# A rewritten opening of a two-layer mixture kernel: adapter merges in pairs of batches, conditioned chunks split from PSUM, gating lagged by one chunk

## The reference

```python
hidden_i = x @ wi.T + 2 * (x @ common_wi_a.T) @ common_wi_b.T + expert_lora(x, ids)     # 128 -> 512
cur = relu(hidden_i) @ wo.T + the same two corrections                                   # 512 -> 128
for r in range(4):
    logits = cur @ Wg[r] + bg[r]
    cw = softmax over the two largest of four logits, zero elsewhere
    y[e] = gelu(cur @ W1[e] + b1[e]) @ W2[e] + b2[e]
    cur = cur + sum_e cw[e] * y[e]
x = x + cur
x = x + ffn(lora_by_language(x))
```

## Time and profile before

| | us |
|---|---|
| median of 3 runs | 513.68 (512.76 to 515.19) |
| profiled execution, its own time | 512.37 |
| its span, first to last instruction | 510.6 |

### The profile page before, as it was taken

The page is one execution under the profiler, slowest core; times in us unless marked ns, Lnnn a source line. Parts: engine busy times, 40 slices in busy tenths (PEclk is TensorE's granted clock), DMA queues, the critical chain, the costliest instruction groups (busy, mean ns, idle before and its releaser), DMA issues.

```text
span 510.6 us, 7414 instructions
## 1 busy us (share of the span) xinstructions
PE 499.0 (98%) x2268; PEld 406.0 (80%) x2268; DVE 417.3 (82%) x606; ACT 391.6 (77%) x541; POOL 124.8 (24%) x103
## 2 busy tenths in 40 slices
PE   9989799999999999999999999999999999999997
PEld 7867688778788888778888877888888788788885
DVE  3578999999999999999999999999987567744333
ACT  2454598779788877979888787988888787698653
POOL 3576712122121212112131211214232334310000
PEclk8899999999999999999999999999999999999999
DMA  7700170202022020202202020230202000000001
GB/s 211 189 5 1 39 313 1 84 1 85 0 85 82 1 83 0 83 0 83 82 1 83 0 83 0 83 120 6 83 1 83 1 0 1 1 0 1 0 22 64
DMA packets 6746, 26.30 MB, mean 52 GB/s; under 512 B 2178, under 2 KB 2562, under 8 KB 4546
## 3 DMA queue, kind: packets, MB, share of 16 engines
q1 hardware_dynamic: 6434, 23.11, 13.3%
q0 software_dynamic: 288, 2.88, 1.6%
HBM read 24.81 MB, written 1.18 MB: 51 GB/s over the span
## 4 chain that ended last, share of the span: by engine, by line
PE 53%; DVE 22%; issue 13%; ACT 10%; DVEq 1%; POOL 1%; ACTq 0%; POOLq 0%
PE bank L413 19%; PE bank L414 18%; PE bank L417 11%; ACT act_out L696 6%; DVE hid_lo L923 6%; DVE prod L934 3%; ACT hid_hi L702 3%; DVE chosen L899 2%; PE bank L474 2%; PE bank L441 1%; PE bank L436 1%; DVE logit_lo L870 1%; DVE turned L868 1%; DVE ffn_lo L983 1%; DVE hid_lo L1022 1%
## 5 line engine op out<-in xcount | busy, mean ns | idle before, releaser
L696 ACT ACTIVATE act_out<-bank,vec 128x512 f32<-128x512 f32 x256 | 162.7, 680 | 47.9 <-DVE hid_lo L923 23.7
L923 DVE TENSOR_TENSOR hid_lo<-act_out,hid_hi 128x1024 fp32r<-128x1024 f32 x128 | 161.6, 1283 | 21.5 <-ACT hid_hi L702 21.5
L702 ACT ACTIVATE hid_hi<-act_out 128x1024 fp32r<-128x1024 f32 x128 | 135.9, 1062 | 7.9
L378 POOL TENSOR_TENSOR cur<-cur,prod 128x512 f32<-128x512 f32 x48 | 65.9, 1374 | 240.1 <-DVE prod L934 239.7
L413 PE MATMUL bank<-hid_hi,moe_hi 128*128 128x512 f32 x256 | 100.8, 394 | 2.7 <-DVE hid_lo L923 1.9
L417 PE MATMUL bank<-hid_hi,moe_lo 128*128 128x512 f32 x256 | 99.8, 390 | 0.0
L414 PE MATMUL bank<-hid_lo,moe_hi 128*128 128x512 f32 x256 | 99.7, 390 | 0.0
L414 PE MATMUL bank<-xlo,moe_hi 128*128 128x512 f32 x256 | 99.6, 389 | 0.0
L413 PE MATMUL bank<-xhi,moe_hi 128*128 128x512 f32 x256 | 99.6, 389 | 0.0
L417 PE MATMUL bank<-xhi,moe_lo 128*128 128x512 f32 x256 | 99.6, 389 | 0.0
L413 PEld LDWEIGHTS bank<-hid_hi,moe_hi 128*128 128x128 f32 x256 | 48.0, 188 | 16.9 <-DVE hid_lo L923 4.9
(11 more groups left out here) (118 smaller groups left out, 618.8 us busy)
## 6 DMA issues: line engine op xcount, KB each, us to landing
cw_all<-cw_dram SPq DMA_DIRECT2D x16, 1024.0 KB, 4.7
stage<-ffn_w POOLq DMA_DIRECT2D x1, 2304.0 KB, 9.9
cw_all<-moe_w SPq DMA_DIRECT2D x4, 512.0 KB, 8.3
stage<-lora_all SPq DMA_DIRECT2D x8, 160.0 KB, 7.7
x<-x_t SPq DMA_DIRECT2D x4, 256.0 KB, 6.8
out_t<-x SPq DMA_DIRECT2D x3, 256.0 KB, 2.8
cur<-cond_base SPq DMA_DIRECT2D x1, 512.0 KB, 3.2
stage<-ffn_w POOLq DMA_DIRECT2D x1, 512.0 KB, 4.0
```

The costliest lines, as they stand in the source:

```text
L378: pool.tensor_tensor(cur[:, c, :], cur[:, c, :], prod[:, s % 2, :], ALU.add).then_inc(add_done, 1)
L696: act.activation(act_out[:, f // 2, f % 2, :], bank[:, f, :], ACT.Gelu_apprx_tanh, bias=vec[:, V_B1 + e * FC + f:V_B1 + e * FC + f + 1]).t ...
L702: act.activation(hid_hi[:, s % 2, f - 1:f + 1, :], act_out[:, f // 2, :, :], ACT.Copy)\
L923: dve.tensor_tensor(hid_lo[:, s % 2, 2 * pr:2 * pr + 2, :], act_out[:, pr, :, :], hid_hi[:, s % 2, 2 * pr:2 * pr + 2, :].bitcast(F32), ALU ...
```

## The change

- TensorE merges two batches of one kind at a time (`merge_pair`); the first six merges (kind 0 and kind 1 of batches 0 and 1, kind 0 of batches 2 and 3) stand ahead of the first H and use six banks (6, 7, 4, 5, 2, 3). Then for each pair p: H, H, two merges of kind 1, O, O, two merges of kind 0. The diff below calls merges k, with `merge_of(k)` giving batch and kind.
- The inputs' first chunk and the base weights go over ScalarE's queue; the mixture weights are asked for after all low-rank factors.
- Merged weights pass through six scratch rows (act_out and prod); the language factors load into free rows of `stage`.
- `conditioned(c)` writes `xhi` first; the low part is taken by VectorE from PSUM, no longer by GpSimd from `cur`.
- Gating is one chunk later: `gate_order` for chunk c+2 at e = 3, `gate_choice` for chunk c+1 at e = 0, tanh inside ScalarE's work of e = 1, `gate_weights` at e = 1. The opening does two gate_order, one gate_choice and one gate_weights, where before it did three, three and two.
- GpSimd asks for the FFN weights after its last `moe_lo`.

```diff
-LOAD_AFTER = [0, 1, 3, 4]
-MOE_AT = {0: [0], 1: [1], 2: [2], 3: [3], 5: [4, 5], 6: [6, 7]}
+LOAD_AFTER = {3: 1, 5: 2, 7: 3}
+PAIRS = BATCHES // 2
+FIRST_MERGES = 6
+SCRATCH = 6
...
+            for k in range(0, FIRST_MERGES, 2):
+                merge_pair(k)
+                warm(KEEP_WARM)
+            for p in range(PAIRS):
+                cond_hidden(2 * p)
+                cond_hidden(2 * p + 1)
+                if p < PAIRS - 1:
+                    merge_pair(4 * p + 6)
+                if p == 1:
+                    pe.wait_ge(wg_done, 1)
+                    pe.wait_ge(xs_done, 1)
+                    logits(0, GATE_FIRST)
...
+            def merge_pair(k):
+                b, kind = merge_of(k)
+                if k >= FIRST_MERGES:
+                    pe.wait_ge(merge_free, merge_before(k + 1) + 1)
+                pe.wait_ge(lora_in[b], 16)
+                pe.wait_ge(lora_in[b + 1], 16)
...
+            def conditioned_low(c):
+                dve.wait_ge(cond_xhi, c + 1)
+                dve.wait_ge(cond_cur, c + 1)
+                dve.tensor_tensor(xlo[:, c, :], bank[:, cond_bank(c), :], xhi[:, c, :].bitcast(F32), ALU.subtract)\
+                   .then_inc(xs_done, 1)
...
+            for p in range(PAIRS):
+                relu_low(2 * p)
+                relu_low(2 * p + 1)
+                for k in range(4 * p + 6, min(4 * p + 8, MERGES)):
+                    merged_sum(k)
+                if p + 2 < CHUNKS:
+                    x0_low(p + 2)
+                if p == 0:
                     split_gate()
+                if p == 1:
+                    dve.wait_ge(const_done, CONSTS)
+                    gate_order(0, 0)
+                if p == 2:
+                    gate_choice(0)
+                if p == 3:
+                    gate_weights(0, True)
+                for k in range(4 * p + 8, min(4 * p + 10, MERGES)):
+                    merged_sum(k)
+                if p < CHUNKS - 1:
+                    conditioned_low(p)
+            gate_order(1, 0)
+            conditioned_low(CHUNKS - 1)
             hidden_low(0, 0)
-            gate_choice(CHUNKS - 2)
```

More of the change, by code:

```diff
@@ L367, in mixture_add @@
+            for k in range(FIRST_MERGES):
+                merged_low(k)
+            for p in range(PAIRS):
+                for half, i in enumerate(moe_pieces(p)):
+                    for k in range(4 * p + 2 * half + 6, min(4 * p + 2 * half + 8, 2 * BATCHES)):
+                        merged_low(k)
+                    moe_low(i)
             def mixture_add(rnd, s, last):
@@ new lines, in merge_pair @@
+            def merge_pair(k):
+                b, kind = merge_of(k)
+                if k >= FIRST_MERGES:
+                    pe.wait_ge(merge_free, merge_before(k + 1) + 1)
+                pe.wait_ge(lora_in[b], 16)
+                pe.wait_ge(lora_in[b + 1], 16)
+                for i in range(2):
+                    for fc in range(FC if kind else 1):
+                        rows, half = lora_rows(b + i), b // 4
+                        if kind == 0:
+                            mm = pe.matmul(bank[:, merge_bank(k + i), :], lora[rows, half, 0:D], lora[rows, half, D:D + F],
+                                           start=True, stop=True)
+                        else:
+                            a = D + F + fc * P
+                            mm = pe.matmul(bank[:, merge_bank(k + i), fc * D:(fc + 1) * D], lora[rows, half, a:a + P],
+                                           lora[rows, half, D + 2 * F:LORA_W], start=True, stop=True)
+                        if fc == (FC - 1 if kind else 0):
+                            mm.then_inc(merge_done, 1)
@@ L687, in tanh_gate, with hidden @@
                 act.activation(tanh_gap[:], half_gap[:], ACT.Tanh).then_inc(tanh_done, 1)
-            def hidden(n, s, first=False):
+            def hidden(n, s, first=False, gate=None):
                 e = s % EXPERTS
@@ L703, in hidden @@
                            .then_inc(hi_done, 1)
+                    if f == 1 and gate is not None:
+                        tanh_gate(gate)
             def project_high(c):
@@ new lines, in _ @@
+            for k in range(FIRST_MERGES):
+                merged_high(k)
+                if k == 3:
+                    x0_high(1)
+            for p in range(PAIRS):
+                relu_high(2 * p)
+                relu_high(2 * p + 1)
+                for half, i in enumerate(moe_pieces(p)):
+                    for k in range(4 * p + 2 * half + 6, min(4 * p + 2 * half + 8, MERGES)):
+                        merged_high(k)
+                    moe_high(i)
+                    if half == 0 and p + 2 < CHUNKS:
+                        x0_high(p + 2)
+                if p == 2:
+                    tanh_gate(0)
+                if p < CHUNKS - 1:
+                    conditioned(p)
@@ L943, in round_steps @@
                     n, c, e = STEPS * rnd + s, s // EXPERTS, s % EXPERTS
-                    if s <= EXPERTS + 1:
-                        if e == 1:
-                            gate_weights(CHUNKS * rnd + CHUNKS - 2 + c)
-                    elif e == 1 and not last:
-                        gate_weights(CHUNKS * (rnd + 1) + c - 2)
                     if s < STEPS - 1:
@@ L953, in round_steps @@
                         hidden_low(n + 1, 0)
+                    gated = not (last and c == CHUNKS - 1)
+                    if e == 1 and gated:
+                        gate_weights(CHUNKS * rnd + c + 1)
                     if last and e == 1 and c >= 1:
```

344 lines of the change are left out of this document (134 added, 210 removed).

## The result

| | before | after |
|---|---|---|
| median, us | 514.43 (4 runs, 512.76 to 515.57) | 539.0 (4 runs, 536.85 to 540.93) |
| ratio | | 1.0479, 95% interval 1.0424 to 1.0534 |
| profiled execution, own time | 512.37 | 540.93 |
| its span | 510.6 | 539.1 |
| first expert_out starts | 68.48 | 74.13 |

The change makes the kernel 4.8% slower, more than three times what was forecast and outside the range. The last two lines split the 28.5 us of span: 5.65 are lost in the opening and 22.9 behind it. From its first FFN matmul to the end layer 1 takes 88.5 us against 88.35, so the rounds lost some 22.7 us.

The account below looks back on a forecast made before the run. PE, busy 98% of the span, was taken as the bound, so only its idle and slow stretches count. 4.7 (opening) + 1.5 (clock) + 1.5 (rounds) = +7.7 on 512.4 gave 520.1; predicted median 520.5, range 510 to 527.

Parts of the forecast that it names:

- The start: Opening up to H(0): PE starts at about 6.9, half clock from 9.8, H(0) ends at 21.7, 2.8 us later than before.
- The pairs: Opening's paired batches: PE waits for VectorE and ScalarE, 2.2 and 2.4 us the longest; expert_out(0) at 73.2, +4.7 with the start.
- The clock again: Opening: idles of 2.2 and 2.4 us within 7 us bring one fall of PE's clock, +1.5 us, bounds 0 and 3.
- The low part from PSUM: Opening, VectorE: the subtraction reading PSUM takes 0.67 us; at 1.37 it would add 2.1 in all.
- The rounds: Rounds: moved gating, with tanh in mid-step, costs 0.1 us a chunk over 14 chunks, +1.5, bounds 0 and +12.
- the rounds suffer: Rival: tanh and gate_order at e = 3 make PE wait 0.9 us a chunk, 531 us; chance 0.13.
- Wrong: PE waits of 10 us or more in the rounds: Sign against the forecast: PE waits of 10 us or more in the rounds, at steps with e = 0 or 1.
- The clock holds: Rival: full clock through the opening's merges makes the start 5.4 us better than in the sum, 514.7 us; chance 0.15.
- the opening paced by PE alone: Rival: VectorE keeps up, so the opening's idles and clock fall vanish, 10.7 us off, 509.4 us; chance 0.14.

Follow-up runs that it names:

- o1: e3 with the loads of base and of chunk 0 of x0 moved back to SP's queue: 515.25 us, ratio 1.005 to the kernel before.
- p1: o1 with gate_order(0) behind low halves of batches 4 and 5, gate_choice(0) behind those of 6 and 7, tanh_gate(0) in the first hidden: 513.28 us.
- e1: The changed kernel with only ScalarE's tanh moved from the middle to the end of its step: 521.07 us, ratio 1.017 to the kernel before.
- e3: The changed kernel with tanh at the step's end and gate_order at e=0, gate_choice at e=1, gate_weights at e=2: 517.94 us, ratio 1.011.
- e4: The kernel before with only its tanh moved, into the middle of ScalarE's step behind gate_choice: 522.36 us, ratio 1.017.
- q1: p1 plus split_gate behind the sums of merges 8 and 9, and WARM, KEEP_WARM = 15, 6 for 12, 2: 510.29 us, ratio 0.993.

## Why the prediction was wrong

**The start.** Forecast: half rate from 9.8, clock near 0.5 from 10 to 20 us, H(0) at 19. Measured: 0.50 and 0.50, H(0) at 19.25. That the time is right is luck: two errors cancel. PE was to start at 6.9 and started at 9.04, as the landing was taken from before at 2.7 although x0 and base went to another queue, and o1 shows that this move nearly doubled it. Against that the merges were too dear in the sum. It had 3.8 us for any two at half rate; to the next instruction the pair of kind 1 took 3.03 (12.19 to 15.22) and the second pair of kind 0 took 2.01 (16.37 to 18.38), together 2.6 less. The two merges of the row behind the price were of two kinds and one batch, and the new order puts two batches of one kind side by side.

**The pairs.** H(4) was to start at 42.9 and started at 44.04. Idle ahead of M14: 2.2 forecast, 0.41 measured; ahead of O(4): 2.4 and 2.67; ahead of expert_in: 1.7 and 1.44. The chain is the one described: gate_order(0) on VectorE ahead of sums 12 and 13, and relu_high behind two merged_high on ScalarE; p1, which takes gate_order out of it, has 1.6 us less idle ahead of O(4). The first expert_out was to come at 73.2 (+4.7) and came at 74.13 (+5.65). **The clock again** was to add 1.5. The fall that it was charged for came, at 52.8 behind O(4)'s idle. But the one from 35 us, which before has as well, was twice as long: 0.58 from 35 to 40 us and 0.74 from 40 to 45, 3.4 us of clock, where before had 0.83 over the ten, 1.7. From 24 us to the first expert_out the clock was 0.90 in after and 0.96 in before, 5.0 us against 1.8. The two terms together are 6.2 against 5.65 measured, with errors on both sides in them: the clock cost twice the 1.5, the idles about M10 and the logits were 2.3 in place of 1.0, M14's was 1.8 too long, and the five pairs of merges from M6 to M15 were taken at 2.1 to 2.2 each and took 1.63 and 1.06 in turn, some 3.4 us less, an estimate from the rows above. The chain held; that its sum came within 0.6 us is in part luck, and two profiles of this one opening differ by 1.7.

**The low part from PSUM** was taken at 0.67. It took 0.69. VectorE's timeline after, PSUM's subtraction and then an input's with two SBUF operands:

```profile
35.68 0.69 DVE L879 TENSOR_TENSOR xlo<-bank,xhi 128x512 fp32r<-128x512 f32 x1 [2.26 <-ACT cur L763]
...
41.81 1.48 DVE L856 TENSOR_TENSOR xlo<-x,xhi 128x512 fp32r<-128x512 f32 x1 [1.74 <-ACT xhi L756]
```

**The rounds** are the step that failed. The sum had 0.1 us a chunk over 14 chunks, +1.5, with bounds 0 and +12. Measured: +22.7, of which 1.2 us a chunk, some 18 over the 15 tanhs, and the rest once in the last round, with 3.4 us of clock missing and 2.5 more of PE's wait for GpSimd, which overlap in part. The rival *the rounds suffer* named the tanh together with gate_order, took 0.9 a chunk and gave 531 with 0.13; it had the right mechanism at three quarters of its price and nothing for the last round. The sum went by VectorE's load: 8.4 us of work at e=3 against PE's 5.6. That load was real and was worth 2 to 4 us (e1 to e3). The tanh was dismissed in one sentence without being priced by a row. Its sign could have been seen: a step is four gelus and two high parts on ScalarE (1.23 for two gelus and 1.06 for a high part in the rows above), 4.6 us of PE's 5.6, so it leaves about 1.0; gate_choice, six instructions, takes 2.3 us (199.37 to 201.64) and starts behind the product of the step. A wait of 1.55 us in the middle of ScalarE's step is larger than its slack and comes back every chunk; at the end of the step the same tanh finds its input ready (0.9 us of waiting in all the rounds). It is not the instruction, 0.26 us, but what stands behind it. The size does not come out of this: 1.55 less 1.0 is 0.6 us a chunk, an estimate that lies between the 0.4 of e4 and the 1.2 of after. "Wrong: PE waits of 10 us or more in the rounds" came true: 8.3 for ScalarE, 4.0 and 3.2 for the others, and more on PEld.

**The rivals** of the other side fell with it. *The clock holds* had no case in `after` itself (0.50), *the opening paced by PE alone* neither. They return in part in p1 and q1, with the tanh, the loads and VectorE's order mended (and more warming in q1): the clock is 1.00 from 10 to 20 us and the new opening ends at 65.16 and 65.85, under the 68.48 of the earlier trace rows and the 71.26 of e4. PE still has 5 to 7 us of idle and a fall of the clock behind 24 us in both, so it is not paced by PE alone.

One more thing in the sum: it gives 520.1 for the profiled execution, and with the 1.3 by which the median lay higher that is 521.4, not the 520.5 predicted. Nothing hangs on it here.

## What to carry to other kernels

A small instruction that waits across engines must be priced by what stands behind it in its own engine's queue, not by its duration: put it where that engine's step ends, and compare the wait with the step's slack, once for every pass of the loop. The slack tells here whether it hurts, not how much. When a block of small instructions makes a neighbour late, spread it over gaps; set down whole at the next place, it took 1.6 us off one idle and added 4.5 to the next. When a load goes to another queue, look at the landing of the loads behind it, not only at its own issue. And before a few us of an opening are put down to an edit, compare two profiles of the same opening: here they differ by 1.7 and 2.8 us.
